# Gram stage of a two-block image kernel: fp32 rows are turned directly, split when copied out of the bank, and GpSimd takes over most of the normalising

## The chip, the cores and the metric

One core of a Trainium2 chip runs the whole program. The metric is the device time of one execution in microseconds (us), lower is better; for several runs the median is given. Engines: PE is TensorE (PEld its weight loads), DVE VectorE, ACT ScalarE, POOL GpSimd, SP SyncE.

## What is computed

The input is an image batch of shape (2, 128, 128, 96). Two residual blocks follow each other, each on a group-normalised input (32 groups of 3 channels); the second is what this change touches:

```python
motif = patches.reshape(B, G, Cg * 9, L).reshape(B, G, 9, Cg, L)   # the nine 3x3 shifts of 16 groups
gram = jnp.einsum('bgjcl,bgjdl->bgjcd', motif, motif)
sq = jnp.einsum('bgjcl,bgjcl->bgjc', motif, motif)
d2 = sq[..., :, None] + sq[..., None, :] - 2.0 * gram
nn_idx = jnp.argmin(jnp.where(eye, jnp.inf, d2), axis=-1)
...
x = x + _L0_conv_ref(_gn(x), ...)
x = x + _L1_conv_ref(_gn(x))
```

Only the order of the distances `d2` within a group matters for what is picked, so a common factor on all grams changes nothing.

## The kernel before, in words

For each of the two images (b = 0, 1) the program runs attention (L954 and around it), then the gram stage `motif_grams`, then `motif_terms`, which gathers planes and adds the terms. Stages are blocks with their own instruction streams per engine; the order of work inside the gram stage is the order in which each engine's function issues it, tied together by semaphores.

In the gram stage the image lies in SBUF as `img`: 128 partitions (one image axis) by 128 by 96 channels in fp32, so that neighbours of the inner image axis are 96 numbers apart. It is normalised in place by groups of 3 channels, eight pieces of 12 channels. The stage then works in 48 units of two channels each.

- ACT makes an fp16 high half of a piece (`high_first`, `high`, L1219 and L1225) in `split`, POOL subtracts it from the piece to make the fp16 remainder (L1209); for the first piece DVE does this (`low_first`, L1414). `split` is laid out as 130 columns by 12 channels, two slots; its last two columns are zeros, so that each turn loads a full 128 columns.
- `turn(u)` on PE (L1285): 12 transposes of 128 x 128 fp16, 6 for the high half into one bank, 6 for the remainder into another (2 channels by 3 shifts each). The weight load takes the strided column of `split`, the moving operand is a contiguous identity.
- `out(u)`: ACT copies the high bank to `turned_hi` (L1232), DVE the remainder bank times 2 to `turned_lo` (L1429). The two run beside each other.
- `gram(m)` on PE (L1304): 32 matmuls of 128 x 120 fp16, two for each of 16 groups, accumulate high x high and high x 2 remainder into four banks. A gram is issued two units (`LAG`) behind the turn that it needs; 31 grams stand among 48 units, 29 of them before the last turn has been copied out. The first stands behind turn 4.
- `last_column` (L1316, L1322) waits for the copies of the last unit, and the rest of the grams follow it.
- There are two banks of each kind, so `turn(u)` waits until unit u - 2 has been copied out.

On DVE the other work of the stage stands between the copies: normalising the pieces (L1407, L1420), for b = 0 the statistics of the next image (L91, in 9 of each 12 units), for b = 1 the sums for the output from unit 17 on, every second unit (`sum_rows`, L1466 and L1471). SP saves the normalised image once all pieces are done. Ten matmuls with zeros (L1268) keep PE at work until the first piece is there.

Of the kernel before, what the change touches and what calls it, by code (L numbers as in the profile page):

```python
# [413 lines left out]
def attention(nc, b, k, x, img, shared, v_dram, x1_rows, x1_out, sems):  # L414
# [13 lines left out]
    with ExitStack() as ctx:  # L428
# [505 lines left out]
        def _(pe):  # L934
# [127 lines left out]
            for n in range(1, UNITS):  # L1062
# [15 lines left out]
GRAM_SEMS = ("m_ready", "m_summed", "m_rooted", "m_dve", "m_set_up", "m_normed", "m_hi", "m_lo", "turned_h", "turned_l",  # L1078
             "out_h", "out_l", "chunk_done", "f_out", "grams_out", "post_pe", "post_act", "picks", "picks_spread",
             "pick_pe", "grams_out2", "next_in", "next_stats", "lo_first", "sum_done", "sum_out0", "sum_out1")  # L1080


def motif_grams(nc, b, k, img, shared, fc_ahead, x_after, f_dram, x1_rows, x1_out, att_sems, sems):
# [16 lines left out]
    with ExitStack() as ctx:  # L1100
        sb = lambda n, s, d: ctx.enter_context(nc.sbuf_tensor(f"{n}{b}", s, d))
        split = [sb(f"split{s}_", [P, 2, XP, PIECE], F16) for s in range(2)]

# [3 lines left out]
        if b > 0:  # L1107
# [22 lines left out]
        bank = [ctx.enter_context(nc.psum_tensor(f"ps_m{j}_{b}", [P, 512], F32)) for j in range(8)]  # L1130
        acc, ps_hi, ps_lo = bank[0:4], bank[4:6], bank[6:8]
        ps_s, ps_t, ps_a = bank[7], bank[4:7], bank[0:2]
        (ready, summed, rooted, own, set_up, normed, hi_done, lo_done, turn_hi, turn_lo, out_hi, out_lo, chunk_done,
         f_out, gram_out, post_pe, post_act, picks, picks_spread, pick_pe, gram_out2, next_in,
         next_stats, lo_first, sum_done, *sum_out) = (sems[n] for n in GRAM_SEMS)
        SUM_ROWS, SUM_PART = 8, 16
        NORM_EVERY = 6 if b == 0 else 3
# [10 lines left out]
        half = lambda j, h: split[j % 2][:, h, 0:W, :]  # L1148
        six = lambda t: t[:].bitcast(F16)[0:HM, 0:6 * P].rearrange("p (j g c) -> p j g c", g=MG, c=MC)

        def columns(t, col):

            v = t[0:HM, 0:TCOLS].rearrange("p (g j c) -> p j g c", g=MG, c=MC)
            return v[:, 3 * col:3 * col + 6]
# [44 lines left out]
        def _(pool):  # L1199
# [4 lines left out]
            for s in range(2):  # L1204
                nc.gpsimd.memset(split[s][:, :, W:XP, :].rearrange("p h x c -> p h (x c)"), 0.0).then_inc(set_up, 1)
                nc.gpsimd.memset(turned_hi[s][0:HM, TCOLS:TCOLS + MC], 0.0).then_inc(set_up, 1)
            for j in range(1, PIECES):
                pool.wait_ge(hi_done, j + 2)
                nc.gpsimd.tensor_tensor(half(j, 1), piece(j), half(j, 0), ALU.subtract).then_inc(lo_done, 1)  # L1209

        @block.scalar
        def _(act):
# [3 lines left out]
            def high_first(h):  # L1216
                act.wait_ge(normed, h + 1)
                cols = slice(HALF * h, HALF * h + HALF)
                nc.scalar.activation(split[0][:, 0, 0:W, cols], img[:, :, cols], ACT.Copy).then_inc(hi_done, 1)  # L1219

            def high(j):
                act.wait_ge(normed, j + 2)
                if j >= 2:
                    act.wait_ge(turn_lo, PER_PIECE * (j - 1))
                nc.scalar.activation(half(j, 0), piece(j), ACT.Copy).then_inc(hi_done, 1)  # L1225

            def out(u):
                act.wait_ge(turn_hi, u + 1)
                for q, col in places(u):
                    if q >= 2:  # L1230
                        act.wait_ge(chunk_done, q - 1)
                    last = nc.scalar.activation(columns(turned_hi[q % 2], col), six(ps_hi[u % 2]), ACT.Copy)  # L1232
                last.then_inc(out_hi, 1)

            high_first(0)
            high_first(1)
            high(1)
            for u in range(UNITS):
                out(u)
                if u % PER_PIECE == PER_PIECE - 1 and u // PER_PIECE + 2 < PIECES:  # L1240
                    high(u // PER_PIECE + 2)
# [16 lines left out]
        def _(pe):  # L1258
# [12 lines left out]
            def turn(u):  # L1271
                if u == 0:
                    pe.wait_ge(set_up, 4 if b == 0 else 13)
                if u < PER_PIECE and u % (PER_PIECE // 2) == 0:
                    pe.wait_ge(hi_done, u // (PER_PIECE // 2) + 1)
                    pe.wait_ge(lo_first, u // (PER_PIECE // 2) + 1)
                if u >= PER_PIECE and u % PER_PIECE == 0:
                    pe.wait_ge(hi_done, u // PER_PIECE + 2)
                    pe.wait_ge(lo_done, u // PER_PIECE)
# [108 lines left out]
        def _(dve):  # L1388
# [22 lines left out]
            def low_first(h):  # L1411
                dve.wait_ge(hi_done, h + 1)
                cols = slice(HALF * h, HALF * h + HALF)
                nc.vector.tensor_tensor(split[0][:, 1, 0:W, cols], img[:, :, cols], split[0][:, 0, 0:W, cols],  # L1414
                                        ALU.subtract).then_inc(lo_first, 1)

# [459 lines left out]
```

## Time and profile before

| what | value |
|---|---|
| median of 3 runs | 1435.72 us (1435.39 to 1443.61) |
| the profiled execution, its own time | 1433.58 us |
| span in its profile | 1431.8 us |
| PE busy | 1297.3 us (91%) |
| DVE busy | 1115.2 us (78%) |
| ACT busy | 881.8 us (62%) |
| POOL busy | 632.9 us (44%) |
| mean granted TensorE clock | 0.965 of full |

The profile is of one execution; its span begins with the first instruction and ends with the last, and 1.8 us of the device time lie outside it. The gram stage of image 0 runs from about 351 to 470 us of the span, that of image 1 from about 1045 to 1160 us. A duration of a PE row is the time from an instruction's start to its modelled end; since matmuls overlap, the pace of a sequence is read from the starts.

### The profile page before, as it was taken

The numbers are of one execution on the slowest core, as the hardware profiler recorded it, in microseconds if no ns is written. First come the engines' busy times: TensorE is split into PE (matmuls) and PEld (weight loads), VectorE is DVE, ScalarE is ACT, GpSimd is POOL, SyncE is SP. The second block draws the span as 40 slices with busy tenths as digits, with TensorE's granted clock in tenths as the row PEclk, the third lists the DMA queues.
The fourth block names the chain that finished last, engine by engine and source line by source line (L and its number), as shares of the span: only waits on it lengthen the run. The fifth ranks groups of instructions, "written<-read, shape, count | busy, mean of one in ns | idle before, by whom it ended". The sixth has DMA issues, their size and how long they took to land. (4 is left out here: it accounts for less than half of the span.)

```text
span 1431.8 us, 34123 instructions
## 1 busy us (share of the span) xinstructions
PE 1297.3 (91%) x13586; PEld 1051.1 (73%) x13586; DVE 1115.2 (78%) x1890; ACT 881.8 (62%) x1013; POOL 632.9 (44%) x668
## 2 busy tenths in 40 slices
PE   3899999987899599999989999999869959999998
PEld 1799997986899355555549999989859955555554
DVE  6587775468774499999976777746877839999998
ACT  3567663212553399999965666532145419999996
POOL 4789992332220144434019998714422113444400
PEclk9999999998999799999999999999979979999999
DMA  6466731793125244553536887319205235264433
GB/s 218 121 198 213 225 103 41 234 268 128 52 82 230 102 151 105 162 138 101 124 105 199 265 253 214 89 57 288 73 2 233 103 134 156 84 182 113 147 74 106
DMA packets 77173, 210.28 MB, mean 147 GB/s; under 512 B 15450, under 2 KB 15558, under 8 KB 74326
## 3 DMA queue, kind: packets, MB, share of 16 engines
q1 hardware_dynamic: 62510, 158.10, 34.7%
q0 software_dynamic: 6720, 36.93, 9.7%
q10 hardware_dynamic: 7784, 13.07, 3.3%
q8 instruction: 107, 1.75, 0.5%
q14 instruction: 52, 0.43, 0.1%
HBM read 91.54 MB, written 67.04 MB: 111 GB/s over the span
## 5 line engine op out<-in xcount | busy, mean ns | idle before, releaser
L1801 PE MATMUL acc<-rnd,ident 128*128 128x376 f32 (+1 forms) x1152 | 387.2, 479 | 19.4 <-ACT rnd L1780 19.4
L1801 PEld LDWEIGHTS acc<-rnd,ident 128*128 128x128 f32 x1152 | 215.9, 192 | 137.8 <-ACT rnd L1780 20.7
L954 PE MATMUL ps_a<-wa,shared 128*128 128x192 f16 x1536 | 296.3, 246 | 3.1 <-DMA xc<-low 2.5
L954 PE MATMUL ps_a<-wb,xb 128*128 128x192 f16 x1536 | 295.3, 246 | 0.0
L1775 ACT ACTIVATE rnd_m<-prod,plus_round,scale 128x1504 f32<-128x1504 f32 (+2 forms) x144 | 232.9, 1618 | 56.1 <-DVE prod L1631 49.3
L1740 DVE SCALAR_TENSOR_TENSOR over<-prod,scale,rnd 128x1504 bf16<-128x1504 f32 (+2 forms) x144 | 252.7, 1757 | 0.0
L572 POOL TENSOR_TENSOR vt<-z 96x256 f32<-96x256 f32 x248 | 240.4, 990 | 4.2 <-ACT z L848 4.0
L1780 ACT ACTIVATE rnd<-rnd_m,minus_round 128x1504 f32<-128x1504 f32 (+2 forms) x144 | 220.4, 1531 | 4.7
L1688 POOL DMA_INDIRECT near<-f_planes,index x42 | 119.3, 2840 | 192.9 <-DVE prod L1631 140.4
L954 PE MATMUL ps_a<-wfa,shared 128*128 128x96 f16 x1536 | 157.3, 206 | 4.6 <-issue 4.3
L954 PE MATMUL ps_a<-wfb,xb 128*128 128x96 f16 x1536 | 157.3, 206 | 0.6 <-issue 0.6
L954 PEld LDWEIGHTS ps_a<-wa,shared 128*128 128x128 f16 x1536 | 150.6, 98 | 4.5 <-DMA xc<-low 3.2
L954 PEld LDWEIGHTS ps_a<-wb,xb 128*128 128x128 f16 x1536 | 150.6, 98 | 0.1
L954 PEld LDWEIGHTS ps_a<-wfa,shared 128*128 128x128 f16 x1536 | 140.6, 98 | 2.5 <-issue 2.5
L954 PEld LDWEIGHTS ps_a<-wfb,xb 128*128 128x128 f16 x1536 | 138.3, 98 | 3.4 <-issue 3.4
L1631 DVE TENSOR_TENSOR prod<-shared,img 128x1504 f32<-128x1504 f32 (+2 forms) x72 | 122.2, 1697 | 15.4 <-DMA img<-near 8.0
L1631 DVE TENSOR_TENSOR prod<-shared,near 128x1504 f32<-128x1504 f32 (+2 forms) x72 | 122.3, 1699 | 14.3 <-DMA near<-near 7.6
L638 DVE TENSOR_TENSOR qk<-y_s,qk 128x384 f16<-128x384 f32 x128 | 100.2, 783 | 41.3 <-ACT qk L873 41.3
L954 PE MATMUL ps_a<-wc,xc 102*128 102x192 f16 x512 | 127.2, 248 | 0.0
L1805 PE MATMUL acc<-over,minus_ident 128*128 128x376 bf16 (+1 forms) x576 | 115.5, 323 | 10.8 <-DVE over L1740 9.6
L1805 PEld LDWEIGHTS acc<-over,minus_ident 128*128 128x128 bf16 x576 | 47.6, 98 | 101.0 <-DVE over L1740 73.0
L873 ACT ACTIVATE qk<-y_s 128x384 f16<-128x384 f32 x128 | 67.0, 524 | 85.7 <-DVE y_s L631 83.8
(337 smaller groups left out, 2460.0 us busy)
## 6 DMA issues: line engine op xcount, KB each, us to landing
xb<-shared ACTq DMA_DIRECT2D x64, 195.0 KB, 2.8
f_planes<-img SPq DMA_DIRECT2D x8, 1536.0 KB, 14.3
shared<-f_planes SPq DMA_DIRECT2D x16, 768.0 KB, 5.8
v_a<-shared SPq DMA_DIRECT2D x40, 260.0 KB, 2.6
v_b<-xb SPq DMA_DIRECT2D x40, 260.0 KB, 3.0
shared<-v_a SPq DMA_DIRECT2D x40, 260.0 KB, 4.7
xb<-v_b SPq DMA_DIRECT2D x40, 260.0 KB, 5.3
v_c<-xc SPq DMA_DIRECT2D x40, 195.0 KB, 3.4
```

The lines of the kernel that those rows point to most:

```text
L572: last = nc.gpsimd.tensor_tensor(out[:, i], row(p_), row(q_), op)
L638: nc.vector.tensor_tensor(qk[:, n % 4, :, C2:2 * C2], y[:, n % 2], qk[:, n % 4, :, 0:C2], ALU.subtract).then_inc(qk_lo, 1)
L873: nc.scalar.activation(qk[:, n % 4, :, 0:C2], y[:, n % 2], ACT.Copy).then_inc(qk_hi, 1)
L954: mm = lambda a, w, first, end: nc.tensor.matmul(out(i), a, w, start=first, stop=end)
L1631: return vec.tensor_tensor(prod[:, n % PRODS, lo:hi], fv, nv, ALU.mult)
L1688: pool.indirect_dma_start((near2 if second else near)[:, s, cells], None, f_dram.rearrange("y (e o) -> (y e) o", o=1), bass.IndirectOffset ...
L1740: nc.vector.scalar_tensor_tensor(over[:, n % 2, rows], prod[:, n % PRODS, rows], scale[:, sh:sh + 1], rnd[:, n % RNDS, rows], ALU.mult, AL ...
L1775: nc.scalar.activation(rnd_m[:, n % 2, rows], prod[:, n % PRODS, rows], ACT.Identity, bias=k["plus_round"][:, 0:1], scale=scale[:, sh:sh + ...
L1780: nc.scalar.activation(rnd[:, n % RNDS, rows], rnd_m[:, n % 2, rows], ACT.Identity, bias=k["minus_round"][:, 0:1]).then_inc(rnd_done, 1)
L1801: nc.tensor.matmul(o(m, a, e), k["ident"][:, :], rnd[:, n % RNDS, BR * m + a:BR * m + e, :], start=False, stop=False, skip_group_check=True)
L1805: last = nc.tensor.matmul(o(m, a, e), k["minus_ident"][:, :], over[:, n % 2, BR * m + a:BR * m + e, :], start=False, stop=(sh == KK - 1), ...
```

## The change

`split` and the passes that fill it are gone. Each unit turns its two channels straight from `img` in fp32: six transposes, weight load 126 columns of `img` (96 numbers apart), moving operand the fp32 identity, each channel's three shifts into one bank of a pair. ACT copies both banks of the pair with scale 0.5 into `turned_hi` in fp16; after that DVE makes the remainder, bank minus twice `turned_hi`, in two instructions, one for each bank. DVE normalises pieces 0 and 1, POOL the other six, without a wait between them. The columns of a group in `turned_hi` and `turned_lo` now stand channel by channel, with 8 shifted numbers of each of three shifts inside.

```diff
-            for j in range(1, PIECES):
-                pool.wait_ge(hi_done, j + 2)
-                nc.gpsimd.tensor_tensor(half(j, 1), piece(j), half(j, 0), ALU.subtract).then_inc(lo_done, 1)
+            pool.wait_ge(normed, 3)
+            for j in range(2, PIECES):
+                for g in range(PIECE // GC * j, PIECE // GC * (j + 1)):
+                    fg = img[:, :, GC * g:GC * g + GC]
+                    last = nc.gpsimd.tensor_scalar(fg, fg, mom[:, 0, g:g + 1], mom[:, 1, g:g + 1], ALU.subtract,
+                                                   ALU.mult)
+                last.then_inc(normed, 1)
...
-                act.wait_ge(turn_hi, u + 1)
+                act.wait_ge(turned, u + 1)
...
-                    last = nc.scalar.activation(columns(turned_hi[q % 2], col), six(ps_hi[u % 2]), ACT.Copy)
+                    last = nc.scalar.activation(columns(turned_hi[q % 2], col), channels(u), ACT.Copy, scale=0.5)
...
-                for h, ps, out_, done in ((0, ps_hi, out_hi, turn_hi), (1, ps_lo, out_lo, turn_lo)):
-                    if u >= 2:
-                        pe.wait_ge(out_, u - 1)
-                    for j in range(6):
-                        c_, ki = 2 * u + j // 3, j % 3
-                        last = nc.tensor.transpose(ps[u % 2][:].bitcast(F16)[:, P * j:P * j + P],
-                                                   split[(u // PER_PIECE) % 2][:, h, ki:ki + W, c_ % PIECE],
-                                                   k["ident16"][:, :])
-                    last.then_inc(done, 1)
+                if u >= 2:
+                    pe.wait_ge(out_hi, u - 1)
+                    pe.wait_ge(out_lo, u - 1)
+                for j in range(6):
+                    c_, ki = 2 * u + j // 3, j % 3
+                    last = nc.tensor.transpose(of_channel(u, j // 3)[:, :, MC * ki:MC * ki + MC],
+                                               img[:, ki:ki + HM, c_], k["ident"][:, :])
+                last.then_inc(turned, 1)
...
-                dve.wait_ge(turn_lo, u + 1)
+                dve.wait_ge(out_hi, u + 1)
...
-                    last = nc.vector.tensor_scalar(columns(turned_lo[q % 2], col), six(ps_lo[u % 2]), 2.0, None,
-                                                   ALU.mult)
+                    for h in range(2):
+                        of = lambda t: columns(t[q % 2], col)[:, h]
+                        last = nc.vector.scalar_tensor_tensor(of(turned_lo), of(turned_hi), -2.0, of_channel(u, h),
+                                                              ALU.mult, ALU.add)
...
-            low_first(0)
-            low_first(1)
...
-                if u % NORM_EVERY == 0 and u // NORM_EVERY + 2 < PIECES:
-                    norm(u // NORM_EVERY + 2)
```

How the instructions stand on PE at the beginning of the stage, before (`ps_m_0` are the banks, `split_0` the halves, `ident` the identity; L1285 are the transposes of units 0 to 4):

```order
L1260 MATMUL ps_m_0<-sums,mean_ones 128x64
L1262 MATMUL ps_m_0<-sums,mean_ones 128x64
L1265 MATMUL ps_m_0<-zeros_k 128x480 x4
L1268 MATMUL ps_m_0<-zeros_k 128x480 x10
L1285 MATMUL ps_m_0<-ident,split_0 128x128 x60
L1304 MATMUL ps_m_0<-shared 128x120
```

and the same place on PE after the change (L1271 are the transposes, L1289 the grams):

```order
L1248 MATMUL ps_m_0<-sums,mean_ones 128x64
L1250 MATMUL ps_m_0<-sums,mean_ones 128x64
L1253 MATMUL ps_m_0<-zeros_k 128x480 x4
L1256 MATMUL ps_m_0<-zeros_k 128x480 x10
L1271 MATMUL ps_m_0<-ident,img 126x16x8 x30
L1289 MATMUL ps_m_0<-shared 128x120
```

The first gram still stands behind five units' turns, which are now 30 transposes instead of 60 and read `img`.

On DVE, from the reciprocal that ends the moments of image 0 to the first copies, before:

```order
L1402 RECIPROCAL m_mom<-m_mom 128x32
L1407 TENSOR_SCALAR img<-img,m_mom 128x128x3 x4
L1414 TENSOR_TENSOR split_0<-img,split_0 128x128x6 x2
L1420 TENSOR_SCALAR img<-img,m_mom 128x128x3 x8
L1429 TENSOR_SCALAR turned_lo_0<-ps_m_0 126x6x16x8
L91 BN_STATS stats<-x_next 128x6 x3
```

and after:

```order
L1387 RECIPROCAL m_mom<-m_mom 128x32
L1392 TENSOR_SCALAR img<-img,m_mom 128x128x3 x4
L1399 TENSOR_SCALAR img<-img,m_mom 128x128x3 x4
L1410 SCALAR_TENSOR_TENSOR turned_lo_0<-shared,ps_m_0 126x16x24 x2
L91 BN_STATS stats<-x_next 128x6 x3
```

Two subtractions and one piece's normalising (four instructions) no longer stand ahead of the first copy; the copy itself has become two instructions that read `turned_hi` (`shared`) and the bank.

On POOL, the difference in the gram stage of image 0 (`-` before, `+` after):

```order
-L1205 MEMSET split_0 128x2x24
-L1206 MEMSET turned_hi_0 126x8
-L1209 TENSOR_TENSOR split_0<-img,split_0 128x1536 x7
...
+L1205 MEMSET turned_hi_0 126x8
+L1211 TENSOR_SCALAR img<-img,m_mom 128x128x3 x24
```

Seven subtractions of whole pieces give way to 24 normalising instructions of 384 numbers per partition.

## Rows read from the trace of the kernel before

**Rows 1.** Windows: length; PE, PEld, DVE, ACT, POOL busy (x); clock; DMA share; GB/s.

```profile
364.40:450.50 86.10, 81.98 (x1446) 81.06 (x1445) 60.08 (x183) 44.21 (x53) 19.55 (x6) 1.00 0.37 138
1059.00:1142.50 83.50, 82.88 (x1471) 82.75 (x1468) 66.16 (x102) 45.21 (x54) 21.11 (x6) 0.99 0.35 144
```

**Rows 2.** Timeline of PE: starts of grams, turns and the last column.

```profile
364.38 0.31 PE L1304 MATMUL ps_m<-shared 126*128 126x120 f16 x1
...
400.42 0.91 PE L1285 MATMUL ps_m<-ident,split 128*128 128x128 f16 x12
401.16 0.22 PE L1304 MATMUL ps_m<-turned_hi 126*128 126x120 f16 x1
...
402.84 1.32 PE L1285 MATMUL ps_m<-ident,split 128*128 128x128 f16 x19
...
450.51 0.71 PE L1316 MATMUL ps_m<-zeros_k 128*72 128x432 bf16 x3 [0.74 <-DVE turned_lo L1429]
...
1061.44 0.22 PE L1304 MATMUL ps_m<-shared 126*128 126x120 f16 x1
...
1142.62 0.71 PE L1316 MATMUL ps_m<-zeros_k 128*72 128x432 bf16 x3 [0.74 <-DVE turned_lo L1429]
```

**Rows 3.** Weight loads: by shape (mean ns), and by line (min/median/max ns).

```profile
L1801 PEld LDWEIGHTS acc<-rnd,ident 128*128 128x128 f32 x1152 | 215.9, 192 | 137.8 <-ACT rnd L1780 20.7 <-issue 3.5
L1304 PEld LDWEIGHTS ps_m<-shared 126*128 126x128 f16 x512 | 50.3, 98 | 0.0
...
L1361 PEld LDWEIGHTS ps_m<-order,g_half x192: 139/145/145, 463.2 to 1158.1; 120*72 120x72 f32 x192
L947 PEld LDWEIGHTS ps_w<-ident,img x254: 123/127/204, 39.3 to 902.1; 128*96 128x96 f32 x127
L988 PEld LDWEIGHTS ps_g<-qk x512: 119/123/126, 60.3 to 940.0; 128*96 128x96 f16 x171
L1285 PEld LDWEIGHTS ps_m<-ident,split x1152: 137/145/169, 356.2 to 1141.6; 128*128 128x128 f16 x192
```

**Rows 4.** The turns' weight loads at half clock, another line's range, and the window.

```profile
L1285 PEld LDWEIGHTS ps_m<-ident,split x26: 142/168/169, 361.4 to 364.0; 128*128 128x128 f16 x26
...
L1002 PEld LDWEIGHTS ps_g<-zeros_k x24: 123/123/204, 46.6 to 754.3; 128*96 128x96 bf16 x24
...
361.50:364.00 2.50, 2.50 (x27) 2.50 (x26) 2.50 (x12) 1.66 (x4) 1.91 (x1) 0.50 0.00 0
```

**Rows 5.** Timeline of PE: the last column's matmuls, strided moving operand.

```profile
451.17 0.31 PE L1322 MATMUL ps_m<-turned_hi,turned_lo 126*72 126x72 f16 x1
451.30 0.31 PE L1322 MATMUL ps_m<-turned_hi 126*72 126x72 f16 x1
```

**Rows 6.** Timeline of PE in attention: four fp32 transposes with contiguous weights, then others.

```profile
83.01 0.60 PE L947 MATMUL ps_w<-ident,img 128*96 128x128 f32 x4
83.45 0.49 PE L988 MATMUL ps_g<-qk 128*96 128x192 f16 x4
```

**Rows 7.** Copying and POOL operations nearest to the new ones.

```profile
L742 DVE SCALAR_TENSOR_TENSOR img<-ps_a,img x64: 540/558/559, 258.0 to 1035.5; 128x384 f32<-128x384 f32 x64
...
L1253 ACT ACTIVATE g_turn<-ps_m 72x432 f32<-72x432 f32 x4 | 2.1, 527 | 8.9 <-PE ps_m L1361 8.9
...
L1209 POOL TENSOR_TENSOR split<-img,split x14: 3177/3352/3699, 360.2 to 1121.5; 128x1536 f16<-128x1536 f32 x14
```

**Rows 8.** DVE's other work in the stage, by line (min/median/max ns).

```profile
L1420 DVE TENSOR_SCALAR img<-img,m_mom x56: 453/514/3422, 356.9 to 1082.5; 128x384 f32<-128x384 f32 x56
...
L1466 DVE TENSOR_TENSOR x_sum<-img,gain x20: 248/948/2794, 1086.8 to 1143.2; 128x768 f32<-128x768 f32 x14, 128x96 f32<-128x96 f32 x4, 128x576 f32<-128x576 f32 x2
...
L1471 DVE TENSOR_TENSOR x_sum<-x_sum,mean_c x16: 957/958/960, 1087.9 to 1143.5; 128x768 f32<-128x768 f32 x16
```

**Rows 9.** Timeline of PE: the zeros ahead of the first turn, images 0 and 1.

```profile
353.15 2.94 PE L1268 MATMUL ps_m<-zeros_k 128*128 128x480 bf16 x10
...
1047.01 4.16 PE L1268 MATMUL ps_m<-zeros_k 128*128 128x480 bf16 x10
```

More of the change, by code:

```diff
@@ L1075, in _ @@
                                      ).then_inc(pivot_out, 1)
-GRAM_SEMS = ("m_ready", "m_summed", "m_rooted", "m_dve", "m_set_up", "m_normed", "m_hi", "m_lo", "turned_h", "turned_l",
+GRAM_SEMS = ("m_ready", "m_summed", "m_rooted", "m_dve", "m_set_up", "m_normed", "m_turned",
              "out_h", "out_l", "chunk_done", "f_out", "grams_out", "post_pe", "post_act", "picks", "picks_spread",
-             "pick_pe", "grams_out2", "next_in", "next_stats", "lo_first", "sum_done", "sum_out0", "sum_out1")
+             "pick_pe", "grams_out2", "next_in", "next_stats", "sum_done", "sum_out0", "sum_out1")
 def motif_grams(nc, b, k, img, shared, fc_ahead, x_after, f_dram, x1_rows, x1_out, att_sems, sems):
@@ L1101, in motif_grams @@
         sb = lambda n, s, d: ctx.enter_context(nc.sbuf_tensor(f"{n}{b}", s, d))
-        split = [sb(f"split{s}_", [P, 2, XP, PIECE], F16) for s in range(2)]
         turned_hi = [shared[:, 0:TCOLS + 8], sb("turned_hi1_", [P, TCOLS + 8], F16)]
@@ L1129, in motif_grams @@
                 .rearrange("p (h v j) -> p h v j", h=2, v=3))
-        bank = [ctx.enter_context(nc.psum_tensor(f"ps_m{j}_{b}", [P, 512], F32)) for j in range(8)]
-        acc, ps_hi, ps_lo = bank[0:4], bank[4:6], bank[6:8]
+        bank = [ctx.enter_context(nc.psum_tensor(f"ps_m{j}_{b}", [P, 512], F32)) for j in range(4)]
+        pair = [ctx.enter_context(nc.psum_tensor(f"ps_m{j}_{b}", [P, 1024], F32)) for j in (4, 6)]
+        bank += [t[:, 512 * h:512 * h + 512] for t in pair for h in range(2)]
+        acc = bank[0:4]
         ps_s, ps_t, ps_a = bank[7], bank[4:7], bank[0:2]
-        (ready, summed, rooted, own, set_up, normed, hi_done, lo_done, turn_hi, turn_lo, out_hi, out_lo, chunk_done,
+        (ready, summed, rooted, own, set_up, normed, turned, out_hi, out_lo, chunk_done,
          f_out, gram_out, post_pe, post_act, picks, picks_spread, pick_pe, gram_out2, next_in,
-         next_stats, lo_first, sum_done, *sum_out) = (sems[n] for n in GRAM_SEMS)
+         next_stats, sum_done, *sum_out) = (sems[n] for n in GRAM_SEMS)
         SUM_ROWS, SUM_PART = 8, 16
-        NORM_EVERY = 6 if b == 0 else 3
         SUM_FIRST = UNITS - 2 * (H // SUM_ROWS) + 1
@@ L1147, in motif_grams @@
         piece = lambda j: img[:, :, PIECE * j:PIECE * j + PIECE]
-        half = lambda j, h: split[j % 2][:, h, 0:W, :]
-        six = lambda t: t[:].bitcast(F16)[0:HM, 0:6 * P].rearrange("p (j g c) -> p j g c", g=MG, c=MC)
+        of_channel = lambda u, h: pair[u % 2][0:HM, 512 * h:512 * h + 3 * P].rearrange("p (g k) -> p g k", g=MG)
+        channels = lambda u: (pair[u % 2][0:HM, :].rearrange("p (h e) -> p h e", h=2)[:, :, 0:3 * P]
+                              .rearrange("p h (g k) -> p h g k", g=MG))
         def columns(t, col):
-            v = t[0:HM, 0:TCOLS].rearrange("p (g j c) -> p j g c", g=MG, c=MC)
-            return v[:, 3 * col:3 * col + 6]
+            v = t[0:HM, 0:TCOLS].rearrange("p (g k) -> p g k", g=MG)[:, :, CK * col:CK * col + 2 * CK]
+            return v.rearrange("p g (h k) -> p h g k", h=2)
         def places(u):
@@ L1214, in _ @@
             nc.scalar.activation(mom[:, 1, :], part[:, 1, :], ACT.Sqrt, bias=k["eps"][:, 0:1]).then_inc(rooted, 1)
[L1216 to L1225, printed above, removed]
             def out(u):
-                act.wait_ge(turn_hi, u + 1)
+                act.wait_ge(turned, u + 1)
                 for q, col in places(u):
@@ L1272, in turn @@
                 if u == 0:
[L1273 removed]
+                    pe.wait_ge(set_up, 2 if b == 0 else 11)
                 if u < PER_PIECE and u % (PER_PIECE // 2) == 0:
[L1275 to L1276 removed]
+                    pe.wait_ge(normed, u // (PER_PIECE // 2) + 1)
                 if u >= PER_PIECE and u % PER_PIECE == 0:
[L1278 to L1288 removed]
+                    pe.wait_ge(normed, u // PER_PIECE + 2)
+                if u >= 2:
[6 more added lines that the diff above has]
+                last.then_inc(turned, 1)
             def first_need(m):
@@ L1409, in norm_half @@
                 last.then_inc(normed, 1)
[L1411 to L1415, printed above, removed]
             def norm(j):
```

6 lines of the change are left out of this document (removed).

## The prediction

> **What bounds the stage now.** I read the windows of the gram stage first. Between the first gram and the last column PE is busy for 82.0 of 86.1 us (image 0) and 82.9 of 83.5 us (image 1), at full clock, while DVE works 60 and 66 us, ACT 44 to 45 and POOL 20 to 21 [rows 1]. So PE sets the pace, and what the change does to PE's own work decides; a relief of DVE, ACT or POOL is worth only the few us for which PE waits for them. The timeline gives PE's pace. Twelve transposes of a unit start at 400.42 and the gram behind them at 401.16: 0.74 us, or 61.7 ns each. The gram's 32 matmuls last from 401.16 to 402.84: 52.5 ns each [rows 2]. Check: behind the first gram stand the turns of units 5 to 47, 43 x 12 = 516 transposes, 31.8 us, and 29 grams, 928 matmuls, 48.7 us, then the 0.74 us wait ahead of the last column: 81.3 us. Image 1 took 1142.62 - 1061.44 = 81.2 us, image 0 450.51 - 364.38 = 86.1 us [rows 2]; the 4.9 us more are waits in the middle. The model stands.
>
> **The one number that matters: an fp32 turn with a strided weight load.** Half as many transposes help only if one costs less than 2 x 61.7 = 123 ns. A turn's pace is the longer of two things that overlap, its moving pass and its weight load.
>
> The moving pass is in the trace. Four fp32 transposes that move the same 128-column identity take 83.45 - 83.01 = 0.44 us, 110 ns each [rows 6]. They load contiguous rows of `img`, though. The new turns load 126 numbers that are 384 bytes apart.
>
> The load has to be worked out. Ordinary fp32 loads of 72 and 128 contiguous columns last 145 and 192 ns [rows 3]: 47 ns for 56 columns, 0.84 ns a column (two clocks), on a fixed part of 85 ns. The fp32 transposes' loads of 96 columns (127 ns) and fp16 loads of 96 columns (123 ns) fit that fixed part with 0.42 ns a column, one clock. But 128 contiguous fp16 columns take only 98 ns [rows 3], 13 ns above the fixed part: about four columns a clock. So a full-width fp16 load is on a faster path, which neither the 96-column loads nor the fp32 ones show.
>
> The turns of before are strided (24 bytes apart) and last 145 ns instead of 98 [rows 3]. Have they lost the fast path? At half clock they last 168 ns, where 96 slow contiguous columns reach 204 [rows 4]. So they are still on it, and the stride costs them time: 145 - 85 = 60 ns for 128 columns taken four at a time, 32 steps of 1.88 ns. The last column shows the same figure on one stream: its moving operand, 72 fp16 numbers of which each lies 48 bytes or more from the one before it, takes 451.30 - 451.17 = 0.13 us, 1.82 ns a number [rows 5], over four clocks for each. Two rows, one price: about 1.8 to 1.9 ns for each number read far from the last one, on each stream.
>
> The new load is fp32, has 126 columns, and has one stream by these rows. 126 x 1.82 = 229 ns, 126 x 1.88 = 237 ns; if some 11 ns of the 131 in the last column are fixed, 210 ns. The bounds for a turn are 110 ns (the stride costs nothing, the moving pass decides) and 237 ns plus a few for the hand-over. I take 230 ns, because both strided rows give it and the 110 ns row is of contiguous loads.
>
> The Trainium skill has a rule for each half of this. "Advanced Engine Details and Errata", section Memory Cachelines, says that SBUF is read in 16-byte lines and that at least two hits on a line are needed to hide the access; every number of the new load is on a line of its own. By that rule alone no size follows; rows 5 give it. "TensorE: Matmul & The Clock Gate", section Weight-path perf modes, says that the fast load wants 128 weights and no fp32. The new turns have neither; the 98 and 123 ns of rows 3 agree for fp16, and no row has a strided fp32 load.
>
> **The parts.**
> - Turns: 43 x 6 = 258 behind the first gram. 258 x 0.230 = 59.3 us instead of 31.8.
> - Grams: unchanged, 48.7 us.
> - Copies: ACT reads 768 fp32 numbers. The 432-number copy from a bank took 527 ns [rows 7]; at some 0.83 ns a number 768 take 0.81 us, as now. DVE's remainder is two instructions of 384 numbers with one operand in a bank and one in SBUF; the nearest row has the same form and 540 to 559 ns over 64 instructions, though POOL works there too [rows 7]. I take 1.1 us for both; an ACT copy of 1.1 us or a DVE one of 0.8 each would still be covered at 230 ns a turn. They now stand behind ACT: 0.2 + 0.8 + 1.1 + 0.1 = 2.2 us from the end of a turn to free banks. PE has the next turn (1.38 us) and mostly a gram (1.68 us) in between, 3.1 us. Hidden at 230 ns, with 0.9 us to spare. At 110 ns the cover is 2.3 us and it is no longer hidden everywhere (the rival below).
> - The last unit's copies are not covered: the wait ahead of the last column grows from 0.74 to about 2.1 us, for each image.
> - DVE: the copies cost at most 43 x 1.1 = 47 us of the stretch, where DVE had 26 of 86 us free with the old copies in it [rows 1], and the stretch gets longer; normalising goes, and with it the instructions that took up to 3.42 us where the median is 0.51 [rows 8]. All hidden.
> - POOL: 24 instructions of 384 numbers. From 3.35 us for 1536 numbers [rows 7], 0.84 us each; bounds 0.4 and 1.7. A piece takes 3.4 us (at most 7), and PE uses one up in 6 units, 15 us. Hidden. If they hold up `own_gains` on DVE, then by about one instruction.
> - SP saves the image earlier; nothing on the path waited for it here.
>
> **The sum.** Stretch from the first gram to the last column: 59.3 + 48.7 + 2.1 = 110.1 us. Image 0: 110.1 - 86.1 = +24.0. Image 1: 110.1 - 81.2 = +28.9. Start: the zeros end at about 356.0 and 1051.0 [rows 9]; the first piece's half is normalised by then, and the conversions that PE waited for are gone, so five turns of 1.38 us put the first gram at 362.9 instead of 364.4 (-1.5) and 1057.9 instead of 1061.4 (-3.5). The clock was at half level in 361.5 to 364 [rows 4], and with the first gram earlier it will run part of a gram or all of it at 1.2 GHz: +1.5 each, +3. Behind the last column nothing changes. Total +50.9 us on 1433.6: 1484.5 for that execution. The median of the runs lies 2.1 us above it, so 1487. With 210 ns instead of 230 the 516 turns of both stretches give 10 us less, with 245 ns 8 more, and the clock some 10 more: 1475 to 1505 for this case.
>
> **Rivals.**
> - The stride is free: each fp32 load runs in several streams at once, or the two clocks of the moving pass hide it. This decides below 0.87 ns a column (110 ns for 126). For it: the fp16 turns hide nearly all of their stride, with 61.7 ns a turn. Against: they hide it on the wide path only, and the fp32 load of 96 columns looks like one stream. Price: stretch 28.4 + 48.7 + 2.1 = 79.2, so -6.9 and -2.0; first grams held by DVE's copies, -2.7 and -6.1; clock +3; together -15. Then the new serial copies bite: from unit 17 of image 1 a pair of units costs DVE 0.95 + 0.96 + 4 x 0.56 = 4.1 us [rows 7, 8] against PE's 2 x 0.66 + 2.2 = 3.5, 15 pairs, +9, and some +2 in image 0. Sum -4: 1432, within 1%. If those waits stay away, 1420. This is the rival that ends not slower.
> - A price between: partly overlapped loads, 140 to 180 ns a turn. +8 to +30 us, about 1460. Nothing in the rows asks for it.
> - The clock. By my numbers PE streams columns for 107 of 230 ns in a turn. The stage can lose its clock, as the 0.50 of rows 4 shows. Grams at 1.2 GHz take twice as long; if half of them are hit, +48 us more over both images: 1535. Against: at least one gram mostly stands in any two units, and before held 1.00 with 40% of its PE time in turns [rows 1]. The skill's "TensorE: Matmul & The Clock Gate", section Part 4: PE-mode transpose, says that transposes do not count as busy for the gate; the 1.00 of rows 1 doesn't contradict it, since grams stood between. By that rule the gate would see only grams, 1.7 of 3.1 us, and this rival's 1535 is what would follow.
> - fp32 reads far apart cost more than fp16 ones (twice the bytes): 460 ns a turn, +120 us more.
>
> **Chances.** Strided load on one stream, 1487: 0.66. Price between: 0.06. Clock lost: 0.06. Dearer fp32: 0.02. Stride free: 0.20, of which 0.14 within 1% and 0.06 faster. About 1% is what a measurement of this kernel tells from no change. So slower 0.80, same 0.14, faster 0.06. The likeliest case alone has 1475 to 1505; to leave out no more than 2 in 10 the range goes down to the upper part of the free-stride case and a little into the clock case: 1429 to 1510.
>
> **What would show it.** Right: the transposes' weight loads last about 85 + 230 = 315 ns and start some 230 ns apart; PE is busy nearly throughout, DVE and ACT wait for PE more than before; first gram to last column about 110 us in both images. Wrong: transposes 110 ns apart and PE waiting for DVE's remainders, above all in the second half of image 1. The clock rival shows as a granted clock of 0.50 inside the stretch. If POOL's normalising is dearer than I think, PE waits at a piece's first turn.

## The result: 1447.4 us, 0.8% more than before

The changed kernel takes 1447.42 us (median of 10 runs, 1440.85 to 1460.72), the kernel before 1435.56 us (10 runs beside them). The ratio is 1.0077, its 95% interval 1.0054 to 1.0100: slower, by too little for the bound of 1% and far from the 1487 us forecast. It lies inside the stated range of 1429 to 1510, but that is luck: no case of the prediction had this cause. The profiled execution has a span of 1442.8 us, 11.0 more than before.

### Where the 11 us are

The first two windows of the changed kernel run from first gram to last column, in image 0 and image 1, and answer to [rows 1]; the other two cut the middle of the second one. Columns as there: length, PE, PEld, DVE, ACT, POOL busy with counts, clock, DMA share, GB/s.

```profile
360.20:443.50 83.30, 79.79 (x1188) 78.64 (x1186) 66.34 (x215) 36.67 (x47) 35.05 (x21) 1.00 0.39 146
1050.20:1153.60 103.40, 84.46 (x1188) 82.08 (x1185) 72.98 (x128) 37.05 (x47) 36.53 (x22) 0.93 0.28 116
1079.00:1087.00 8.00, 0.44 (x9) 0.27 (x6) 0.24 (x2) 0.00 (x0) 7.73 (x5) 0.73 0.00 0
1087.00:1095.00 8.00, 5.08 (x49) 5.04 (x50) 7.83 (x15) 1.62 (x2) 0.00 (x0) 0.63 0.95 402
```

Image 0 became faster, 83.3 us instead of 86.1, and image 1 lost 22.3: by the starts below 103.5 instead of 81.2. In that stretch PE is busy for only 84.5 us. From 1079 to 1087 nearly nothing runs but POOL; then the clock is at 0.63 and the DMAs are full. The DMAs were as full in the kernel before, without any loss for PE:

```profile
1087.00:1095.00 8.00, 8.00 (x149) 8.00 (x146) 7.81 (x11) 4.53 (x6) 3.70 (x1) 1.00 1.03 432
```

The timeline of PE in the changed kernel, the starts that answer to [rows 2] and [rows 9]:

```profile
347.39 0.69 PE L1248 MATMUL ps_m<-sums,mean_ones 128*128 128x64 f32 x2 [10.40 <-DVEq L1375]
...
360.17 0.22 PE L1289 MATMUL ps_m<-shared 126*128 126x120 f16 x1
...
380.61 1.54 PE L1271 MATMUL ps_m<-ident,img 128*126 128x128 f32 x12
381.99 0.22 PE L1289 MATMUL ps_m<-turned_hi 126*128 126x120 f16 x1
...
443.51 0.71 PE L1301 MATMUL ps_m<-zeros_k 128*72 128x432 bf16 x3 [2.04 <-DVE turned_lo L1410]
...
1050.17 0.22 PE L1289 MATMUL ps_m<-shared 126*128 126x120 f16 x1
...
1153.65 0.71 PE L1301 MATMUL ps_m<-zeros_k 128*72 128x432 bf16 x3 [2.04 <-DVE turned_lo L1410]
```

Twelve turns in 1.38 us are 115 ns each, so a unit's six cost 0.69 us instead of the 0.74 of its twelve before. The wait ahead of the last column is 2.04 us, forecast 2.1. The first gram of image 1 now comes 11.6 us after the stage's first matmul (1038.60); in before it was 16.9. The sum: the stage of image 0 begins 3.3 us earlier (in code that did not change), -0.9 to the first gram, -2.8 in the stretch, +1.1 from there to the first matmul of image 1's stage, -5.4 to the first gram of image 1, +22.3 in its stretch, and nothing behind it: the 11.0.

The lines of the new instructions, min/median/max in ns:

```profile
L1271 PEld LDWEIGHTS ps_m<-ident,img x576: 184/189/226, 352.9 to 1151.2; 128*126 128x126 f32 x192
...
L1225 ACT ACTIVATE shared<-ps_m x52: 805/810/819, 354.0 to 1127.7; 126x768 f16<-126x768 f32 x52
...
L1410 DVE SCALAR_TENSOR_TENSOR turned_lo<-shared,ps_m x104: 532/546/556, 354.8 to 1130.4; 126x384 f16<-126x384 f16 x104
...
L1211 POOL TENSOR_SCALAR img<-img,m_mom x48: 1636/1850/1929, 353.5 to 1085.1; 128x384 f32<-128x384 f32 x48
...
1044.92 41.81 POOL L1211 TENSOR_SCALAR img<-img,m_mom 128x384 f32<-128x384 f32 x24 [5.73 <-DVE img L1399]
```

The copies cost what the nearest rows said [rows 7]. The weight load lasts 189 ns, not 315. POOL's instructions last about 1.64 or 1.85 us, two of each in a piece; the 24 of image 1 take 41.8 us, 1.74 each. That is at my upper bound of 1.7 (a piece in at most 7 us), and twice the 0.84 that I took.

### The stall in image 1

The timeline of the changed kernel around 1087 us:

```profile
1078.21 8.52 POOL L1211 TENSOR_SCALAR img<-img,m_mom 128x384 f32<-128x384 f32 x5
1086.76 3.06 SPq L1183 DMA_DIRECT2D f_planes<-img  x4
1086.76 1.09 DVE L1447 TENSOR_TENSOR x_sum<-img,gain 128x96 f32<-128x96 f32 x3 [10.30 <-POOL img L1211]
...
1088.77 1.94 DVE L1410 SCALAR_TENSOR_TENSOR turned_lo<-turned_hi,ps_m 126x384 f16<-126x384 f16 x4
1089.92 2.80 PE L1271 MATMUL ps_m<-ident,img 128*126 128x128 f32 x12 [10.49 <-DVE turned_lo L1410]
```

POOL's 24 instructions begin at 1044.9 and end at 1086.8. DVE's first sum stands behind the copy of unit 17 and waits until all pieces are normalised, since it reads whole rows. Behind it in DVE's queue stands the copy that PE waits for. So POOL stops DVE for 10.30 us and DVE stops PE for 10.49; the next turns come at half clock (12 in 2.8 us instead of 1.54), and SP starts saving the image at the same moment. PE waits for DVE for 16.7 us ahead of its turns in the whole stretch, 10.5 of them in this one wait; nothing in image 0 is like it. The waits of DVE in this stage:

```profile
DVE turned_lo L1410 <- ACT shared L1225: 11.2, 9, 2.2
DVE x_sum L1447 <- POOL img L1211: 10.3, 1, 10.3
DVE turned_lo L1410 <- ACT turned_hi L1225: 7.0, 8, 1.4
DVE x_sum L1447 <- DMA out<-x_sum: 2.3, 1, 2.3
```

The last line, a wait for the store of the sums, is not new; it was 1.5 us in before:

```profile
DVE x_sum L1466 <- DMA out<-x_sum: 1.5, 1, 1.5
```

### The profile page after: what moved, and what is told of

It is laid out like the page before. It is cut to its first block and busy times, and to the rows that moved or that the text cites. A ratio compares the mean times of both kernels' runs of the same rounds, so it can differ in the third digit from the quotient of the medians.

```text
span 1442.8 us, 33094 instructions
## 1 busy us (share of the span) xinstructions
PE 1296.3 (90%) x13010; PEld 1047.6 (73%) x13010; DVE 1122.4 (78%) x1940; ACT 860.3 (60%) x995; POOL 669.4 (46%) x698
## 5 line engine op out<-in xcount | busy, mean ns | idle before, releaser
L580 POOL TENSOR_TENSOR td<-side 128x192 f32<-128x192 f32 x128 | 92.3, 721 | 58.7 <-ACT side L866 58.7
```

The lines of the kernel that those rows point to most:

```text
L580: nc.gpsimd.tensor_tensor(td[:, n % 2, 0], side[:, n % 2, 0], side[:, n % 2, 1], ALU.add).then_inc(t_made, 1)
```

## Experiments

Eleven kernels. The program ahead of the gram stage is the same in all of them, and yet that stage began between 345 and 357 us in their profiles; so the length from first gram to last column is the sharper measure, and the time with its interval the final one. The length comes from one profile each. How far it repeats shows where the code is the same: image 0 took 83.3 or 83.4 us in four profiles (after, dve_norm_b1, shared_norm, lumps) and 85.8 in a fifth (few_sums), image 1 91.9 and 90.7 in dve_norm_b1 and dve_norm_all. The kernels pool_runs, strides and widths compute something else and hold PE back until all pieces are normalised; their times, 1514, 1521 and 1533 us, one run each, say nothing of the change, and only the lengths of instructions are read from them.

### Who normalises

**dve_norm_b1.** In image 1 DVE takes the pieces back, one in every three units as in the kernel before.

```diff
+        NORM_EVERY = 6 if b == 0 else 3
...
-            pool.wait_ge(normed, 3)
-            for j in range(2, PIECES):
+            if b == 0:
+              pool.wait_ge(normed, 3)
+              for j in range(2, PIECES):
...
             for u in range(UNITS):
+                if b > 0 and u % NORM_EVERY == 0 and u // NORM_EVERY + 2 < PIECES:
+                    norm(u // NORM_EVERY + 2)
                 out(u)
```

> The changed kernel, but in image 1 DVE normalises the six pieces itself, between its copies, as before the change; GpSimd does so in image 0 only. Theory A (GpSimd's slow normalising stops DVE's sums at unit 17 of image 1, and the rest follows from it): the 10.3 us wait of DVE for GpSimd is gone, image 1 takes 84 to 88 us from first gram to last column instead of 103.5, and the time falls by some 15 us, to about 1432. Theory B (the remainders that stand behind ACT and take two DVE instructions are the cost): DVE has even more to do, image 1 stays at 98 us or more, the time at 1442 or above.

Measured: 1439.25 us, ratio to before 1.0018 (0.9986 to 1.0050). The window of image 1:

```profile
1052.80:1144.70 91.90, 83.94 (x1188) 81.03 (x1187) 80.17 (x146) 37.26 (x47) 0.00 (x0) 0.98 0.32 130
```

91.9 us, 11.5 less than with POOL. It lies between the theories, in neither's range. A is right about the stall; but another 10.7 us stay above the 81.2 of before, about half of the loss, and B is right that something else costs.

**dve_norm_all.** The same for both images.

> DVE normalises all pieces of both images in the places of before; GpSimd does nothing in the stage. Theory A: as with image 1 alone, about 1432, since GpSimd's work costs nothing in image 0 (83.3 us from first gram to last column there stay within 2 us). Theory B: DVE's 24 instructions more in image 0 cost 3 us or more on top of a time that is already above 1442.

Measured: 1444.49 us, ratio 1.0069 (1.0030 to 1.0109). Image 0 goes from 83.3 to 88.4 us, PE's work being the same:

```profile
357.60:446.00 88.40, 81.20 (x1189) 79.14 (x1188) 73.88 (x235) 37.03 (x47) 0.00 (x0) 1.00 0.38 143
```

So in image 0 GpSimd's part of the change is worth 5 us. DVE is busy for 74 of 88 us only: its total is not the bound. PE waits for DVE's copies ahead of turns for 5.1 us there, 1.7 in image 0 of dve_norm_b1, and a wait of 0.5 to 0.8 us follows each of the five rows of four normalising instructions within the stretch (four other waits stand elsewhere). That reads as the row of four holding up a copy; lumps tries the like for the sums.

**act_norm.** ACT normalises, with `scale` and a shift -mean x scale that DVE computes once.

```diff
+            def norm_act(g):
+                fg = img[:, :, GC * g:GC * g + GC]
+                last = nc.scalar.activation(fg, fg, ACT.Identity, scale=mom[:, 1, g:g + 1], bias=shift[:, g:g + 1])
...
                 out(u)
+                per = 1 if b == 0 else 2
+                first = 2 * PIECE // GC + per * (u - 1)
...
+                    for g in range(first, first + per):
+                        norm_act(g)
```

> The changed kernel, but ACT normalises the six pieces, one instruction of 384 numbers behind each copy in image 0 and two in image 1, with a scale and a shift per group. ACT has 40% of its time free there. Theory A: no wait of DVE for GpSimd, no DVE work added; image 1 takes 83 to 86 us from first gram to last column, image 0 83 to 85, the time about 1428 to 1432. Theory B (serial remainders): image 1 stays at 98 us or more, 1442 or above. A delay of ACT's copies by the instructions between them would show as PE waiting in units 1 to 24.

Measured: 1440.28 us, ratio 1.0025 (0.9994 to 1.0056). Image 0 took 84.4 us as expected, image 1 92.1: theory A missed, and B's 98 too. DVE had 6 us less to do there than in dve_norm_b1 (74.1 us busy) and nothing was gained.

```profile
1057.90:1150.00 92.10, 82.67 (x1188) 79.51 (x1186) 74.13 (x129) 49.61 (x68) 0.00 (x0) 1.00 0.32 130
```

**pool_runs.** Why is POOL's instruction so slow?

```diff
-                    fg = img[:, :, GC * g:GC * g + GC]
+                    if b == 0:
+                        fg = img[:, 32 * (g % 4):32 * (g % 4) + 32, PIECE * j:PIECE * j + PIECE]
+                    else:
+                        fg = img[:, 4 * g:4 * g + 4, :].rearrange("p a c -> p (a c)")
```

> The changed kernel; GpSimd's 24 instructions of 384 numbers run over 32 rows of 12 neighbouring channels in image 0 and over 4 whole rows (384 contiguous numbers) in image 1, instead of 128 rows of 3 channels; PE waits for all pieces first, and the values are not the reference's. Theory R (short runs of 3 numbers make the 1.85 us): 0.85 us or less with contiguous rows, between them with runs of 12. Theory O (the operation with two per-partition scalars is slow on GpSimd whatever the layout): 1.8 us in both images.

Measured, image 0 and image 1:

```profile
L1214 POOL TENSOR_SCALAR img<-img,m_mom x24: 1635/1650/1672, 355.8 to 393.3; 128x384 f32<-128x384 f32 x24
...
L1214 POOL TENSOR_SCALAR img<-img,m_mom x24: 1635/1642/1907, 1086.1 to 1123.8; 128x384 f32<-128x384 f32 x24
```

Theory O: 1.64 us with contiguous numbers, 4.3 ns a number with whatever is fixed in it. The two-input subtraction of 1536 numbers that I took as the nearest row costs 2.2 ns a number [rows 7]. The kernel before also has one of 384 numbers, 0.91 us; so at the same size the new operation costs 1.8 times as much. Whether it is the two scalars, the two operations or the fp32 result (this one writes fp16) was not tried.

```profile
L301 POOL TENSOR_TENSOR wqk_lo<-w,wqk_hi x6: 904/912/913, 19.2 to 26.8; 97x384 f16<-97x384 f32 x6
```

The runs of 3 cost nothing for half of the groups. In the changed kernel, while DVE stood still, the last instruction of one piece and the first of the next took 1.64 us, the two behind them 1.85:

```profile
L1211 POOL TENSOR_SCALAR img<-img,m_mom x2: 1636/1637/1638, 1078.2 to 1079.8; 128x384 f32<-128x384 f32 x2
...
L1211 POOL TENSOR_SCALAR img<-img,m_mom x2: 1849/1850/1851, 1081.5 to 1083.3; 128x384 f32<-128x384 f32 x2
```

The dearer two of a piece's four groups are those whose 12 bytes lie across a multiple of 16 in the row of `img`. That this is the reason was not tried apart.

### What a far column costs in a weight load

**before_126.** The kernel before, two columns fewer.

```diff
-                        last = nc.tensor.transpose(ps[u % 2][:].bitcast(F16)[:, P * j:P * j + P],
-                                                   split[(u // PER_PIECE) % 2][:, h, ki:ki + W, c_ % PIECE],
+                        last = nc.tensor.transpose(ps[u % 2][:].bitcast(F16)[0:HM, P * j:P * j + P],
+                                                   split[(u // PER_PIECE) % 2][:, h, ki:ki + HM, c_ % PIECE],
```

> The kernel before, its fp16 turns with 126 columns as weights instead of 128 (the two columns more are zeros that are not used). Theory S of the prediction (a wide fp16 load runs on four streams, and a far column costs 1.88 ns on each): the weight load lasts about 85 + 237 = 320 ns, the pace of turns is 240 ns, over 150 us more. Theory T (a far column costs two clocks, 0.83 ns, on one stream, as the fp32 turns of the changed kernel show with 189 ns): the load lasts about 190 ns, the pace is 105 to 110 ns, some +50 us. Theory U (the stride had taken the turns off the fast path already, at one clock a column): the load stays at 137 to 145 ns, the pace at 62, the time at 1435.

Measured: 1645.34 us, ratio 1.1459 (1.1412 to 1.1507). The load and a unit's turns:

```profile
L1285 PEld LDWEIGHTS ps_m<-ident,split x1152: 292/313/324, 355.0 to 1353.5; 128*126 128x126 f16 x192
...
404.72 2.77 PE L1285 MATMUL ps_m<-ident,split 128*126 128x128 f16 x12
```

Theory S, to a few ns: 313 where it said 320, +209 us where it said over 150. Leaving out two columns of zeros more than doubles the load. Twelve turns take 2.77 us with the last one's 0.38, so 217 ns each, where 240 stood. The reasoning from [rows 3 to 5], that the wide load had four streams and a far fp16 number costs 1.88 ns on each, gives the right length of the load for fp16 at this distance.

**strides.** Then why do fp32 turns not pay it? Turns that read 126 fp32 numbers at distances of 1, 4, 12 and 96 numbers:

```diff
+                    if u % 12 < 3:
+                        last = nc.tensor.transpose(to, flat[:, c_:c_ + HM], k["ident"][:, :])
+                    elif u % 12 < 6:
+                        last = nc.tensor.transpose(to, flat[:, c_:c_ + 4 * HM:4], k["ident"][:, :])
...
```

> The changed kernel with its turns reading other numbers: in each 12 units three read 126 contiguous fp32 numbers, three every 4th, three every 12th, three every 96th as in the change; PE waits for all pieces first, and what is turned is not the reference's. Theory T (far columns cost two clocks, near ones one): loads of 137 ns for the contiguous case, 189 for the three others. Rival V (an fp32 load of this kind costs two clocks a column whatever the stride): 189 for all four. Theory S of the prediction in any form would need the load to grow with the stride. The pace stays at 110 to 116 ns in all, set by the moving pass.

Measured, in the order contiguous, 4, 12, 96:

```profile
L1275 PEld LDWEIGHTS ps_m<-ident,img x144: 137/140/230, 396.8 to 1208.6; 128*126 128x126 f32 x144
...
L1277 PEld LDWEIGHTS ps_m<-ident,img x144: 193/209/230, 401.8 to 1214.9; 128*126 128x126 f32 x144
...
L1279 PEld LDWEIGHTS ps_m<-ident,img x144: 199/218/227, 409.1 to 1221.8; 128*126 128x126 f32 x144
...
L1281 PEld LDWEIGHTS ps_m<-ident,img x144: 184/189/208, 414.9 to 1227.5; 128*126 128x126 f32 x144
```

Distance does cost, 189 against 140 ns, that is (189 - 85) / 126 = 0.83 ns a column instead of 0.44 (an estimate with the prediction's fixed part of 85 ns); but less with 384 bytes than with 16 or 48. Six turns of each kind, in the same order:

```profile
447.95 0.83 PE L1275 MATMUL ps_m<-ident,img 128*126 128x128 f32 x6
...
453.47 0.94 PE L1277 MATMUL ps_m<-ident,img 128*126 128x128 f32 x6
...
457.37 0.97 PE L1279 MATMUL ps_m<-ident,img 128*126 128x128 f32 x6
...
440.16 0.88 PE L1281 MATMUL ps_m<-ident,img 128*126 128x128 f32 x6
```

From start to start of neighbouring turns the medians are 109, 120, 124 and 110 ns. So at 384 bytes the dearer load lies behind the moving pass, as the change needs it; at 16 and 48 bytes it does not, and the expected 110 to 116 in all was a miss. V falls, T holds within 30 ns.

**widths.** The same places of the same image, read as fp32 or as the fp16 half of each number.

```diff
+                    if u % 12 < 6:
+                        a = 2 * C * ki + 2 * c_ + 1
+                        last = nc.tensor.transpose(to[0:HM], halves[:, a:a + 2 * C * (HM - 1) + 1:2 * C],
+                                                   k["ident16"][:, :])
...
```

> The changed kernel; from unit 12 on its turns read other things out of the same image, which are not the reference's: by turns of three units fp32 numbers 384 bytes apart (126 columns), fp16 halves of those numbers 384 bytes apart with 126 columns, the same with 128 columns, and fp16 halves 4 bytes apart with 126 columns. PE waits for all pieces first. Theory W (on one stream a far column costs what its width makes it: 2-byte numbers 1.8 to 1.9 ns, 4-byte ones 0.83 ns): loads of 189, about 315, about 145, and for the 4 bytes apart some 140. Rival D (24 bytes apart are worse than 384, whatever the type): the fp16 loads 384 bytes apart with 126 columns last 190 like the fp32 ones. Rival P (the fp16 transpose itself is slow with 126 columns): 315 at 4 bytes apart as well.

Measured: fp32 at 384 bytes; fp16 at 384 bytes with 126 and with 128 columns; fp16 at 4 bytes:

```profile
L1274 PEld LDWEIGHTS ps_m<-ident,img x60: 184/189/208, 1163.5 to 1220.0; 128*126 128x126 f32 x60
...
L1280 PEld LDWEIGHTS ps_m<-ident,img x54: 287/308/310, 1171.3 to 1227.1; 128*126 128x126 f16 x54
...
L1284 PEld LDWEIGHTS ps_m<-ident,img x54: 167/207/290, 1176.7 to 1233.0; 128*128 128x128 f16 x54
...
L1288 PEld LDWEIGHTS ps_m<-ident,img x54: 134/138/141, 1183.0 to 1238.5; 128*126 128x126 f16 x54
```

Theory W for 126 columns; D and P fall. From one set of places fp16 takes 308 ns and fp32 189: the price of a far number goes with its width, and the narrower one is dearer, 1.77 against 0.83 ns. From start to start the fp16 turns stand 215 ns apart and the fp32 ones 111. The wide fp16 load (207, expected 145) comes between; its shortest is 167. With 128 columns the distance does matter, 145 ns at 24 bytes and 207 at 384, with 126 it does not (313 and 308). Why was not tried. The Trainium skill, "TensorE: Matmul & The Clock Gate", section Weight-path perf modes, asks 128 weights and no fp32 for the fast load; the 308 and 207 ns agree for the columns. The Trainium skill, "Advanced Engine Details and Errata", section Memory Cachelines, has a penalty where each access is on another 16-byte line, and the type decide how far one can stride. The fp32 loads agree with the penalty, 189 to 218 ns against 140.

### What the copies behind each other cost

**few_sums.** From dve_norm_b1, with seven eighths of the sums left out (`rows = [(0, 1, 2)]`, and one row in the addition).

> The kernel with DVE normalising in image 1, and the sums for the output cut to one row of 96 numbers of each eight (seven eighths of them are left out). Theory B2 (what is left of image 1's loss is DVE: two units cost it two copies of 0.93 us and 1.86 us of sums, against 3.5 us of PE): from first gram to last column image 1 falls from 91.9 us to about 83, as image 0; the time by 8 to 9 us. Rival C2 (the loss is in the chain turn, ACT, DVE, PE itself, whatever DVE has besides): 89 us or more.

Measured: 84.1 us in image 1, as B2 said; the time fell less, 1438.41 us, ratio 1.0000 (0.9965 to 1.0035), where dve_norm_b1 had 1.0018. Part of the difference is in the edit: it also clears the whole of `x_sum` on DVE ahead of the first copies (2.6 us). The first gram of image 1 comes 16.8 us after the stage's first matmul instead of 13.9. The rest of the missing 8 to 9 us stays open; the intervals are wide enough to hide it.

```profile
1063.40:1147.50 84.10, 80.52 (x1189) 78.93 (x1187) 60.61 (x145) 36.79 (x47) 0.00 (x0) 1.00 0.35 142
...
1053.95 2.62 DVE L1460 MEMSET x_sum<- 128x3072 f32 x1 [0.71 <-DVE mean_c L1433]
```

**shared_norm.** ACT and POOL share the pieces of image 1, the sums begin at unit 11.

```diff
-        SUM_FIRST = UNITS - 2 * (H // SUM_ROWS) + 1
+        SUM_FIRST = 11
...
+                if b > 0 and 1 <= u <= 8:
...
+                for t in range(H // SUM_ROWS):
+                    if b > 0 and u == SUM_FIRST + 9 * t // 4:
+                        sum_rows(t)
```

> A version meant to keep both gains: image 0 as in the change; in image 1 ACT normalises pieces 2 to 5 (two instructions behind each of the copies of units 1 to 8), GpSimd pieces 6 and 7, and DVE's sums begin at unit 11 and stand 2.25 units apart instead of 2. By theory B2 DVE then has 1.86/2.25 + 0.93 = 1.76 us a unit, as much as PE, so image 1 takes 83 to 87 us from first gram to last column, and the time is 1428 to 1432, ratio 0.995 to 1.0. If ACT's instructions between the copies or the waits of the chain cost more, image 1 stays at 90 or above.

Measured: 1438.67 us, ratio 0.9997 (0.9967 to 1.0027), image 1 at 91.2 us: a miss. DVE is busy for 75.6 of them, so its total is not the bound, and B2 needed another form.

**lumps.** From shared_norm; the two instructions of a sum are taken apart.

```diff
-                c.then_wait(last)
+                c.done(last)
...
+                    if b > 0 and u == SUM_FIRST + 9 * t // 4 + 1:
+                        sum_rest(t)
```

> The version with shared normalising, but each pair of DVE instructions for the sums (1.86 us in one go) is taken apart: the product behind one unit's copy, the addition of the mean behind the next one's. The same DVE work. Theory L (what held image 1 at 91 us in the last run is the lump of 1.86 us that one copy in two has to wait for, in the chain turn, ACT, DVE, turn): 91.2 us from first gram to last column fall to 87 or less. Rival B2 (only DVE's total counts): it stays at 91.

The windows of image 1, shared_norm first:

```profile
1054.30:1145.50 91.20, 82.89 (x1189) 79.61 (x1188) 75.60 (x132) 44.81 (x60) 8.15 (x5) 1.00 0.34 140
```

```profile
1049.10:1136.00 86.90, 81.22 (x1189) 79.12 (x1188) 74.40 (x132) 44.59 (x60) 7.66 (x5) 1.00 0.36 147
```

The same instructions on each engine at the same clock, 4.3 us less: theory L. It is one profile each, but more than the 1.2 us by which image 1 differed between two kernels with the same code there. Time 1432.46 us, ratio 0.9974 (0.9947 to 1.0001), beside 0.9997 (0.9967 to 1.0027) of shared_norm: the same direction, intervals that overlap. DVE's order now, where one instruction of 0.95 us stands ahead of each copy:

```profile
1091.97 0.95 DVE L1457 TENSOR_TENSOR x_sum<-img,gain 128x768 f32<-128x768 f32 x1
1092.84 1.01 DVE L1420 SCALAR_TENSOR_TENSOR turned_lo<-shared,ps_m 126x384 f16<-126x384 f16 x2
1093.77 0.95 DVE L1467 TENSOR_TENSOR x_sum<-x_sum,mean_c 128x768 f32<-128x768 f32 x1
1094.64 1.01 DVE L1420 SCALAR_TENSOR_TENSOR turned_lo<-shared,ps_m 126x384 f16<-126x384 f16 x2
```

**halves.** From lumps; the copies go by channel, half a unit each, on ACT and on DVE.

```diff
-                last.then_inc(turned, 1)
+                    if ki == 2:
+                        last.then_inc(turned, 1)
...
+                for h in range(2):
+                    act.wait_ge(turned, 2 * u + h + 1)
...
+                        last = nc.scalar.activation(columns(turned_hi[q % 2], col)[:, h], of_channel(u, h), ACT.Copy,
+                                                    scale=0.5)
+                    last.then_inc(out_hi, 1)
```

> The same, and the units' copies are pipelined by channel in both images: PE signals after three transposes, ACT copies 384 numbers and signals, DVE makes the remainder of this half while ACT copies the other. The chain from the end of a turn to free banks falls from about 0.14 + 0.81 + 1.0 to some 1.4 us; ACT works some 0.17 us more a unit. Chain theory: image 0 falls from 83.3 to 81, image 1 from 87 or 91 to 83 or 84, the waits ahead of the last column from 2.0 to 1.5 us, the time is 6 to 10 us below the version with shared normalising, about 1429, ratio 0.993. If DVE's total decides, nothing falls.

Image 0 took 82.3 us, image 1 84.0, and the wait ahead of the last column in image 1 was 1.4 us:

```profile
1053.90:1137.90 84.00, 80.29 (x1189) 78.86 (x1187) 74.01 (x132) 47.54 (x108) 8.75 (x6) 1.00 0.37 152
```

The chain theory is right for the stretches within 1.3 us (81 and 83 or 84 were expected) and for the wait (1.5). The time is 1432.13 us, ratio 0.9972 (0.9944 to 1.0000), where 0.993 was expected: a hair under before, and not apart from lumps (0.9974). Both medians lie under those of both kernels; against the changed kernel's 1.0077 the gain is 1.0%, against before it is at the edge of what the runs can tell.

## Why the prediction was wrong

- **The price of a turn: the step that failed.** "I take 230 ns, because both strided rows give it." Both rows were of 2-byte numbers. Measured 115 ns. before_126 shows that the working was right for fp16 (313 ns, forecast 320), the run widths that it does not carry over to fp32 (189 from the places where fp16 takes 308): a far fp32 number costs 0.83 ns, not 1.82 to 1.88. On 258 turns a stretch that was (0.230 - 0.115) x 258 = 30 us too much, twice. The text called the contiguous fp32 row a lower bound and a rival with 0.20, "stride free"; in effect it was that one. The stride is not free, 49 ns on the load, but the 104 ns that lie above the fixed part stay behind the moving pass of 110.
- **POOL.** "0.84 us each; bounds 0.4 and 1.7": 1.74 on average. The nearest row was another operation. The upper bound was about right.
- **The wait that decided.** I priced POOL only against PE's need of a piece each six units, and called it hidden; the sign I named for a dear POOL, PE waiting at a piece's first turn, did not come either. Image 1 has a second reader, `sum_rows`, which waits for the last piece at unit 17, 31.5 us after POOL's start (1076.4 against 1044.9). By the prediction's own numbers 24 x 0.84 = 20 us would have been done in time; its upper bound, 24 x 1.7 = 41 us, would not, and the bound was checked against PE alone. With 41.8 us DVE stood for 10.3. The stall cost 11.5 of the 22.3 us (dve_norm_b1). It also turned "SP saves the image earlier" round in image 1: 48.2 us after the stage's first matmul instead of 38.5.
- **The rival "stride free".** It had -15 us and then +11 for DVE's serial copies, 9 of them in image 1, so stretches of 79.2 + 2 = 81.2 and 79.2 + 9 = 88.2 us. Without the stall (dve_norm_b1) they were 83.3 and 91.9: the direction was right in both, the size 2 and 4 us short, the reason half right. It counted DVE's total over two units; shared_norm and lumps show that the lump ahead of a copy counts. Its 1432 us and the stall together come near the 1447; the prediction had no case with both.
- **The clock.** The +3 us for first grams at half clock did not come: the first gram took 1.68 us in both images, full pace. The clock rival did not come by itself either, 1.00 in image 0. In image 1 the clock fell with the stall, 0.73 in 1079 to 1087 and 0.63 behind it.
- **Right:** PE's own work bounds image 0 (79.8 of 83.3 us); ACT's copy 0.81, DVE's two 1.1 (1.09), the wait at the end 2.1 (2.04), that the first grams come earlier (-0.9 and -5.4 where -1.5 and -3.5 stood).

## What to carry to other kernels

Before carrying a price from one row to a new instruction, ask in what they differ, the width of a number as well as the distance; where the argument hangs on one such price, the contiguous row of the right type deserves more than a fifth of the chance. When work moves to a slower engine, list every reader of its last result and when each comes due, and not only the reader that takes it piece by piece; check the upper bound of its price against each. Between two buffers what counts is the chain from one turn to the next, so a long instruction ahead of a copy costs even on an engine with time to spare; rather put one short one ahead of each copy (4.3 us of 91.2 here).

## What the runs showed of the hardware

- A transpose's weight load with 126 numbers far apart takes 308 to 313 ns in fp16 (24 or 384 bytes apart) and 189 ns in fp32 (384 bytes apart). With neighbours 4 bytes apart it takes 138 ns in fp16 and 140 in fp32.
- 128 instead of 126 columns of fp16 are a different load: 145 against 313 ns in the kernel before, 209 us of its time. At 384 bytes the wide one takes 207 ns.
- For fp32 a distance of 384 bytes (189 ns) is cheaper than 16 or 48 bytes (209 and 218 ns). Turns follow each other every 110, 120 and 124 ns, contiguous ones every 109. Why was not tried.
- GpSimd's operation with two per-partition scalars takes 1.64 us for 384 contiguous fp32 numbers, 1.8 times its two-input subtraction of 384 numbers (0.91). In runs of 3 it takes 1.64 or 1.85 us, by the place of the run.
